# Paired i and g gates, the forget gate last, a new PSUM layout, and the shared expert's low halves on GpSimd

## The chip, the cores and the metric
One core of a Trainium2 chip. The metric is the device time of one execution in microseconds (us). TensorE (PE) multiplies, VectorE (DVE), ScalarE (ACT) and GpSimd (POOL) do elementwise work, SyncE (SP) issues DMAs. Each engine runs its own instruction list in order and waits on semaphores. TensorE and PSUM: a product accumulates in one of eight banks of 512 float32 per partition; GpSimd works on SBUF alone.

## The reference
x is [16, 256, 256] (batch B, time T, features D). Four residual layers follow each other, in float32:

```python
# RNN over T:   h = tanh(h @ Wh + x_t @ Wx + b);                    x = x + hs
# LSTM over T:  z = x_t @ Wx + b + h @ Wh   (4 x 256 columns: i, f, o, g)
#               c = sigmoid(f) * c + sigmoid(i) * tanh(g);  h = sigmoid(o) * tanh(c);  x = x + hs
# MoE:          shared = gelu(x @ sw1 + sb1) @ sw2 + sb2     (256 -> 1024 -> 256)
#               2 of 4 experts per batch row, chosen by a gate on means over T
#               x = x + sum_e w_be * mask_e * expert_e(x) + shared
# adapter:      low-rank matrices made from cond_1024, two products around a gelu;  x = x + out
```

## The kernel before
Float32 accuracy is reached with float16 matmuls: each operand is a high half (HI) and a low half (LO, the rest), and a product is W_hi x_hi + W_lo x_hi + W_hi x_lo. Features lie on the 128 partitions in C = 2 halves; B = 16 columns belong to one time step.

The scan runs in 16 blocks of U = 16 steps. In block `it`, step `u`, the engines' lists hold: LSTM step u of block it; RNN step u of block it+1; pieces of the shared expert over block it-1 as filler for TensorE; input projections for coming steps; in blocks 1 to 8 also a low-rank product (`low_rank`, steps 12 and 13), and in blocks 1 to 13 the splitting of expert weights in steps 1, 5, 7, 9 and 11 (`EXPERT_WINDOWS`). After the scan come the shared expert's last block, the routed experts and the adapter. The order within a step is written out by hand, in the four `block_steps`, one per engine.

LSTM step on TensorE (`lstm_step`, L1348): wait for the new hidden state's high half (`v_hh`); 24 matmuls of 16 columns for the tiles of f, i and g (`FIG_TILES`, L1363); wait for its low half (`v_hl`); 12 more (L1369); then 8 for o, of which four have HI and LO side by side as 32 columns, so that W_hi meets both in one matmul and the two sums lie 256 columns apart (L1374, L1378). The f, i, g sums of four steps (H = 4) share one bank of two (`FIG`), the o sums of eight steps (G = 8) one of two (`OB`). ScalarE takes one tanh over f, i and g from PSUM (`lstm_gates`, L573). VectorE then makes fc = f*c and ig = i*g (L898, L899), adds the two o sums (L901), and makes c (L904); ScalarE takes tanh of o and of c (L580, L582); VectorE makes the new hidden state's high half (L908), its float32 copy (L911), its low half (L913) and the residual add (L917). The sigmoid is a tanh of half the argument.

Ahead of these sums the projections x_t @ Wx are added into the same places, four steps at a time for f, i, g (`fig_x`) and eight for o (`o_x`). From the third use of a bank on, ScalarE writes the gate biases into it first (`seed`, L589).

The shared expert in the scan: `HALVES` says how many halves (three matmuls of 256 columns) TensorE works off in each step; `FILL` is the table made of it, jobs h0, h1, h2, d0, h3, d1, ... (hidden tile m, down tile m), and `done_tiles(u)` are the hidden tiles that end in step u. For these ScalarE makes the float32 gelu in step u (`shared_full`, L621) and its float16 high half in step u+1 (`shared_hi`, L626), both from PSUM; VectorE then makes the low half, 128x256, at the end of step u+1 (`shared_lo`, L868), and TensorE's down product waits for it. Other work at the ends of VectorE's steps: splitting x for the shared expert (L839, L842, in step 0), sums over time (L846), low halves of weights (L775), of low-rank rows (L1015, steps 2 and 4 of blocks 2 to 9), of x for the RNN (L831), and the shared expert's add (L862, step 15).

GpSimd's step (`rnn_step`, L423) belongs to the RNN: its hidden state's low half (L428), the residual add (L430), and in two of four steps the split of x for the LSTM's projections (L442, L445).

Of the kernel before, what the change touches and what calls it, by code (L numbers as in the profile page):

```python
# [54 lines left out]
FIG_TILES = [2, 3, 0, 1, 6, 7]  # L55
O_TILES = [4, 5]


def build_program(nc, a, out, scratch):
    ctx = ExitStack()  # L60
    with ctx:
# [26 lines left out]
        gate_bias = sb("gate_bias", [P, 8 + C], F32)  # L88
# [12 lines left out]
        tfig = sb("tfig", [P, 6, B], F32)  # L101
# [47 lines left out]
        FIG, OB = bank[0:2], bank[2:4]  # L149
# [8 lines left out]
        def late(*shape):  # L158
# [49 lines left out]
            ld_gate_bias p_gate_bias a_fig_seed a_o_seed pe_fig pe_o v_oz a_fig v_ig v_c2 a_tc v_hh v_h2 v_hl v_x2  # L208
            pe_h a_g v_gh v_gl pe_d v_y
# [84 lines left out]
        def _(sp):  # L294
            with nc.allow_non_contiguous_dma(reason="small tables, once"):
# [24 lines left out]
                for i, tile in enumerate(FIG_TILES + O_TILES):  # L320
                    sp.dma_start(gate_bias[:, i:i + 1], a["L1_cond_b"][tile * P:(tile + 1) * P].rearrange("(p o) -> p o", o=1)
                                 ).then_inc(s["ld_gate_bias"], 16)
# [90 lines left out]
        def _(pool):  # L413
# [42 lines left out]
            for part_, scale in ((slice(0, 4), S_LSTM), (slice(4, 6), 2 * S_LSTM), (slice(6, 8), S_LSTM)):  # L456
                nc.gpsimd.tensor_scalar(gate_bias[:, part_], gate_bias[:, part_], scale, None, ALU.mult
                                        ).then_inc(s["p_gate_bias"], 1)
            nc.gpsimd.memset(gate_bias[:, 8:8 + C], 0.0).then_inc(s["p_gate_bias"], 1)
# [3 lines left out]
            for part_ in (HI, LO):  # L463
                split_x1(T // H - 1, part_)

# [50 lines left out]
        def _(act):  # L516
# [53 lines left out]
            def lstm_gates(blk, u):  # L570
                n = blk * U + u
                act.wait_ge(s["pe_fig"], n + 1)
                nc.scalar.activation(tfig[:], FIG[u // H % 2][:, 0:6 * H * B].rearrange(  # L573
                    "p (m t b) -> p m t b", m=6, t=H)[:, :, u % H, :],
                    ACT.Tanh, scale=0.5 / S_LSTM).then_inc(s["a_fig"], 1)
# [8 lines left out]
            def seed(n_read, bank_, tiles, steps, done):  # L584

                act.wait_ge(s["a_tc"], n_read)
                n = (tiles.stop - tiles.start) * steps * B
                act.wait_ge(s["p_gate_bias"], 4)
                nc.scalar.activation(bank_[:, 0:n].rearrange("p (m t) -> p m t", t=steps * B),  # L589
                                     gate_bias[:, tiles].rearrange("p (m o) -> p m o", o=1).to_broadcast(  # L590
                                         [P, tiles.stop - tiles.start, steps * B]), ACT.Copy).then_inc(s[done], 1)

            def seeds(it, u, last):

                if u % H == H - 1 and not (last and u >= U - 2 * H):
                    seed(it * U + u + 1, FIG[u // H % 2], slice(0, 6), H, "a_fig_seed")
                if u == O_SEEDS[0] and it > 0:
                    seed(it * U, OB[1], slice(6, 8 + C), G, "a_o_seed")
                if u == O_SEEDS[1] and not last:
                    seed(it * U + G, OB[0], slice(6, 8 + C), G, "a_o_seed")  # L600
# [7 lines left out]
            def gelu(tile, m, scale, bias, banks):  # L608
                act.wait_ge(s["pe_h"], tile + 1)
                act.wait_ge(s["v_gl"], tile - 1)  # L610
# [30 lines left out]
            def block_steps(it, first, last, matrix=False):  # L641
                for u in range(U):
# [108 lines left out]
        def _(dve):  # L751


            dve.sem_inc(s["v_gl"], M)
# [110 lines left out]
            def shared_lo(tile, m):  # L865
# [3 lines left out]
                                ).then_inc(s["v_gl"], 1)  # L869

            def split_g(tile, m):
# [6 lines left out]
                                ).then_inc(s["v_gl"], 1)  # L878
# [8 lines left out]

            def lstm_step(blk, u, rnn=True):
# [4 lines left out]
                tf, ti, tg = [tfig[:, 2 * k:2 * k + 2, :].rearrange("p c b -> p (c b)") for k in range(3)]  # L893
                x = X[:, :, :, bass.ds(blk * U + u, 1)].rearrange("p c b o -> p (c b o)")
                dve.wait_ge(s["a_fig"], n + 1)
                if n:
                    dve.wait_ge(s["v_c2"], n)
                V.scalar_tensor_tensor(fc[:], tf, 1.0, c2[:], ALU.add, ALU.mult)  # L898
                V.scalar_tensor_tensor(ig[:], ti, 1.0, tg, ALU.add, ALU.mult).then_inc(s["v_ig"], 1)  # L899
                dve.wait_ge(s["pe_o"], n + 1)  # L900
                V.reduce_sum(oz[:], OB[u // G][:, :].rearrange("p (a m t b) -> p m t b a", a=2, m=C, t=G)[:, :, u % G],  # L901
                             AX_X).then_inc(s["v_oz"], 1)
# [115 lines left out]
            def block_steps(it, first, last, xr, matrix=False):  # L1018
                for u in range(U):
                    lstm_step(it, u, not last)  # L1020
                    if last and u in extras:
                        extras[u]()
                    if not first:
# [3 lines left out]
                        for m in done_tiles(u - 1) if u else ():  # L1027
                            shared_lo(it * M + m, m)
# [40 lines left out]
            tail_tile = iter(range(M))  # L1069

# [175 lines left out]
        def _(pe):  # L1246
# [101 lines left out]
            def lstm_step(blk, u):  # L1348
                n = blk * U + u
                old = (u + 1) % 2  # L1350

                def tile_at(bank_, steps, i, tile):
                    at = i * steps * B + u % steps * B
                    return bank_[:, at:at + B], tile

                fig = [tile_at(FIG[u // H % 2], H, i, tile) for i, tile in enumerate(FIG_TILES)]
                o = OB[u // G][:, :].rearrange("p (a m t b) -> p a m t b", a=2, m=C, t=G)[:, :, :, u % G]
                if not isinstance(n, int) or n > 0:
                    pe.wait_ge(s["v_hh"], n)
                for z, tile in fig:  # L1360
                    for c in range(C):
                        for h in (HI, LO):
                            MM(z, LW[:, h, 1, c, tile * P:(tile + 1) * P], LH[:, old, HI, c],  # L1363
                               start=False, stop=False, skip_group_check=True)
                if not isinstance(n, int) or n > 0:
                    pe.wait_ge(s["v_hl"], n)
                for z, tile in fig:
                    for c in range(C):
                        last = MM(z, LW[:, HI, 1, c, tile * P:(tile + 1) * P], LH[:, old, LO, c],  # L1369
                                  start=False, stop=(c == C - 1), skip_group_check=True)  # L1370
                last.then_inc(s["pe_fig"], 1)
                for i, tile in enumerate(O_TILES):
                    for c in range(C):
                        MM(o[:, 0, i], LW[:, LO, 1, c, tile * P:(tile + 1) * P], LH[:, old, HI, c],  # L1374
                           start=False, stop=False, skip_group_check=True)
                for i, tile in enumerate(O_TILES):
                    for c in range(C):
                        last = MM(o[:, :, i], LW[:, HI, 1, c, tile * P:(tile + 1) * P], LH[:, old, :, c],  # L1378
                                  start=False, stop=(c == C - 1), skip_group_check=True)
# [11 lines left out]
            def down_(tile, j, w, first, last_, ybank, halves=range(C)):  # L1391

                if 0 in halves:
                    pe.wait_ge(s["v_gl"], tile + 1)
# [37 lines left out]
            def lstm_x(bank_, i, tile, group, steps, fresh):  # L1432

                n = (steps.stop - steps.start) * B
                z = bank_[:, i * n:(i + 1) * n]
                if fresh:
                    MM(z, bias_pad[:, tile * P:(tile + 1) * P], ones_pad[:, 0:n], start=(i == 0), stop=False,
# [5 lines left out]
            def fig_x(turn, i):  # L1443

                part_ = turn % (U // H)
# [287 lines left out]
```

## Time and profile before
| what | value |
|---|---|
| median of three runs | 1118.36 us (1118.17 to 1118.6) |
| profiled execution | 1117.36 us, span 1115.4 us |
| PE busy | 1079.2 us, 97% of the span |
| DVE, ACT, POOL busy | 818.1, 586.4, 279.3 us |
| mean granted TensorE clock | 0.974 of full speed |

The span runs from the first to the last instruction. A matmul's record lasts longer than the distance to the next one, since matmuls overlap in the array; so the distance between starts is the cost of one, and a busy TensorE may still have room.

### The profile page before, as it was taken

How to read it: one execution, taken by the hardware profiler on the slowest of the kernel's cores; microseconds unless marked ns; L12 is line 12 of the kernel's file. 1: busy time of each engine (PE TensorE's matmuls, PEld its weight loads, DVE VectorE, ACT ScalarE, POOL GpSimd, SP SyncE). 2: the span in 40 equal slices, each digit the busy share in tenths (PEclk: the TensorE clock that was granted, in tenths of full speed). 3: DMA queues.
4: the chain of work that ended last, by engine and by line, in shares of the span. 5: the costliest groups of instructions: out<-in, count | busy, mean ns of one | idle time of the engine just before them, and what ended most of it. 6: DMA issues, size and time to landing. Idle time of an engine off the chain costs nothing. (4 is left out here: it accounts for less than half of the span.)

```text
span 1115.4 us, 54596 instructions
## 1 busy us (share of the span) xinstructions
PE 1079.2 (97%) x21946; PEld 979.4 (88%) x21946; DVE 818.1 (73%) x3458; ACT 586.4 (53%) x2147; POOL 279.3 (25%) x861
## 2 busy tenths in 40 slices
PE   6889999999999999999999998899999999999998
PEld 5889999999999999999999987688888888888877
DVE  7667877877877877777777676686666666676697
ACT  4456666566566566566565543433333333334486
POOL 3523323323333333333333320380000000000041
PEclk8759999999999999999999999999999999999999
DMA  8302120120220100000001110000000000000022
GB/s 258 103 23 59 56 63 25 56 65 23 61 60 26 57 18 29 14 23 23 9 4 27 16 15 12 1 2 2 2 2 2 2 1 2 2 3 2 4 90 82
DMA packets 54913, 36.91 MB, mean 33 GB/s; under 512 B 25560, under 2 KB 53514, under 8 KB 54668
## 3 DMA queue, kind: packets, MB, share of 16 engines
q1 hardware_dynamic: 54060, 33.12, 10.4%
q8 instruction: 181, 2.97, 1.1%
q14 instruction: 64, 0.52, 0.2%
q10 hardware_dynamic: 608, 0.30, 0.1%
HBM read 28.42 MB, written 4.98 MB: 30 GB/s over the span
## 5 line engine op out<-in xcount | busy, mean ns | idle before, releaser
L611 ACT ACTIVATE gel<-bank,seq 128x256 f32<-128x256 f32 x256 | 121.5, 475 | 214.7 <-PE bank L1253 211.9
L1251 PE MATMUL bank<-XHL,WE 128*128 128x256 f16 x768 | 209.9, 273 | 8.2 <-DVE XHL L842 3.4
L1251 PE MATMUL bank<-GH,WE 128*128 128x256 f16 x768 | 209.1, 272 | 2.4 <-DVE GH L868 2.0
L1253 PE MATMUL bank<-XHL,WE 128*128 128x256 f16 x768 | 209.8, 273 | 0.0
L1252 PE MATMUL bank<-XHL,WE 128*128 128x256 f16 x768 | 209.7, 273 | 0.0
L1253 PE MATMUL bank<-GH,WE 128*128 128x256 f16 x768 | 209.4, 273 | 0.0
L1252 PE MATMUL bank<-GH,WE 128*128 128x256 f16 x768 | 209.3, 273 | 0.0
L1363 PE MATMUL bank<-LH,seq 128*128 128x16 f16 x6144 | 194.4, 170 | 9.9 <-DVE LH L908 9.6
L1363 PEld LDWEIGHTS bank<-LH,seq 128*128 128x128 f16 x6144 | 171.5, 96 | 30.1 <-DVE LH L908 14.1
L428 POOL TENSOR_TENSOR RH<-rf,RH 128x32 f16<-128x32 f32 x256 | 63.7, 249 | 420.0 <-ACT RH L568 419.8
L1253 PE MATMUL bank<-seq 128*128 128x64 f16 (+2 forms) x1088 | 163.7, 208 | 0.0
L1252 PE MATMUL bank<-seq 128*128 128x64 f16 (+2 forms) x1088 | 162.4, 207 | 0.0
L1251 PE MATMUL bank<-seq 128*128 128x64 f16 (+2 forms) x1088 | 160.6, 207 | 0.0
L573 ACT ACTIVATE tfig<-bank 128x96 f32<-128x96 f32 x256 | 64.0, 250 | 173.3 <-PE bank L1369 172.3
L875 DVE CAST GH<-gel 128x256 f16<-128x256 f32 x256 | 78.2, 305 | 101.7 <-ACT gel L611 100.8
L877 DVE TENSOR_TENSOR GH<-gel,GH 128x256 f16<-128x256 f32 x256 | 113.0, 441 | 8.7
L898 DVE SCALAR_TENSOR_TENSOR fc<-tfig,c 128x32 f32<-128x32 f32 x256 | 52.1, 203 | 91.8 <-ACT tfig L573 89.2
L1369 PE MATMUL bank<-LH,seq 128*128 128x16 f16 x3072 | 114.2, 169 | 0.0
L1251 PEld LDWEIGHTS bank<-seq 128*128 128x128 f16 x1088 | 104.8, 100 | 3.4 <-issue 0.2
L1252 PEld LDWEIGHTS bank<-seq 128*128 128x128 f16 x1088 | 103.0, 100 | 3.0
L508 POOL TENSOR_TENSOR seq<-X,seq 128x512 f16<-128x512 f32 x16 | 21.4, 1343 | 332.1 <-ACT seq L694 332.1
L1253 PEld LDWEIGHTS bank<-seq 128*128 128x128 f16 x1088 | 103.9, 100 | 0.7
(210 smaller groups left out, 2641.2 us busy)
## 6 DMA issues: line engine op xcount, KB each, us to landing
stage<-in_L_cond_ew SPq DMA_DIRECT2D x64, 128.0 KB, 2.1
stage<-in_L_cond_W SPq DMA_DIRECT2D x32, 256.0 KB, 3.6
XHL<-in_x SPq DMA_DIRECT2D x8, 512.0 KB, 9.0
out<-WE SPq DMA_DIRECT2D x16, 256.0 KB, 2.2
stage<-in_L_cond_sw SPq DMA_DIRECT2D x2, 1024.0 KB, 6.2
scratch<-rows SPq DMA_DIRECT2D x96, 8.0 KB, 2.1
stage<-in_L_cond_Wx SPq DMA_DIRECT2D x1, 1024.0 KB, 9.0
stage<-in_L_cond_Wh SPq DMA_DIRECT2D x1, 1024.0 KB, 11.1
```

Of the source, the lines that this page charges most:

```text
L428: nc.gpsimd.tensor_tensor(RH[:, slot, LO], rf[:, slot], RH[:, slot, HI], ALU.subtract).then_inc(s["p_rlo"], 1)
L508: TT(X3[:, slot, LO], x, X3[:, slot, HI], ALU.subtract).then_inc(s["p_x3"], 1)
L573: nc.scalar.activation(tfig[:], FIG[u // H % 2][:, 0:6 * H * B].rearrange("p (m t b) -> p m t b", m=6, t=H)[:, :, u % H, :], ACT.Tanh, sca ...
L611: nc.scalar.activation(gel[:, m % 2, :], banks[m % len(banks)][:, 0:256], ACT.Gelu_apprx_tanh, scale=scale, bias=bias).then_inc(s["a_g"], 1)
L875: V.tensor_copy(GH[:, m % 4, HI], gel[:, m % 2]).then_inc(s["v_gh"], 1)
L877: V.tensor_tensor(GH[:, m % 4, LO], gel[:, m % 2], GH[:, m % 4, HI], ALU.subtract).then_inc(s["v_gl"], 1)
L898: V.scalar_tensor_tensor(fc[:], tf, 1.0, c2[:], ALU.add, ALU.mult)
L1251: MM(out_, w(HI), x(HI), start=start, stop=False, skip_group_check=True)
L1252: MM(out_, w(LO), x(HI), start=False, stop=False, skip_group_check=True)
L1253: return MM(out_, w(HI), x(LO), start=False, stop=stop, skip_group_check=True)
L1363: MM(z, LW[:, h, 1, c, tile * P:(tile + 1) * P], LH[:, old, HI, c], start=False, stop=False, skip_group_check=True)
L1369: last = MM(z, LW[:, HI, 1, c, tile * P:(tile + 1) * P], LH[:, old, LO, c], start=False, stop=(c == C - 1), skip_group_check=True)
```

## The change
i and g (`IG_TILES`) are now paired as o was: four times two matmuls of 16 columns with W_lo, and after the wait for the low half eight of 32 columns with W_hi on HI and LO side by side. f stays single and is finished after them; o comes last as before. That is 36 matmuls per step instead of 44. The two i, g sums are added by a new VectorE instruction (`lstm_sum`), which stands at the head of VectorE's step; the gate tanh is two, f from PSUM and i, g from SBUF. PSUM: i and g take two banks (four steps each), f and o one bank each, with four and two slots of four steps. The o projections go four steps at a time. Bias seeds: i, g and f and o each every four steps. New waits on TensorE keep a slot's writers and readers apart (`a_f`, `v_oz`, `a_f_seed`, `a_o_seed`). In the scan GpSimd makes the shared expert's low halves, between the RNN's low half and its residual add. `HALVES` is another list.

```diff
-FIG_TILES = [2, 3, 0, 1, 6, 7]
+IG_TILES = [0, 1, 6, 7]
+F_TILES = [2, 3]
 O_TILES = [4, 5]
...
-        FIG, OB = bank[0:2], bank[2:4]
+        IG, FB, OB = bank[0:2], bank[2], bank[3]
...
                 nc.gpsimd.tensor_tensor(RH[:, slot, LO], rf[:, slot], RH[:, slot, HI], ALU.subtract
                                         ).then_inc(s["p_rlo"], 1)
+                if blk > 1 and r > 0:
+                    shared_lo(blk - 1, r)
                 nc.gpsimd.tensor_tensor(x, x, rf[:, slot], ALU.add).then_inc(s["p_x1"], 1)
...
+            def shared_lo(it, u):
+
+                for m in done_tiles(u - 1):
+                    pool.wait_ge(s["a_g"], it * M + m + 1)
+                    nc.gpsimd.tensor_tensor(GH[:, m % 4, LO], gel[:, m % 2], GH[:, m % 4, HI], ALU.subtract
+                                            ).then_inc(s["g_lo"], 1)
...
             def lstm_gates(blk, u):
                 n = blk * U + u
-                act.wait_ge(s["pe_fig"], n + 1)
-                nc.scalar.activation(tfig[:], FIG[u // H % 2][:, 0:6 * H * B].rearrange(
...
+                act.wait_ge(s["pe_f"], n + 1)
...
+                nc.scalar.activation(tf[:].rearrange("p (m b) -> p m b", m=C), z[:, :, u % H], ACT.Tanh,
+                                     scale=0.5 / S_LSTM).then_inc(s["a_f"], 1)
+                act.wait_ge(s["v_zig"], n + 1)
+                nc.scalar.activation(tig[:], zig[:], ACT.Tanh, scale=0.5 / S_LSTM).then_inc(s["a_ig"], 1)
...
+            def seed_f(n):
+
+                turn = n // H
+                if n % H == 2 and 2 <= turn < TURNS - 2:
...
+            def seed_o(n):
+
+                turn = n // H
+                if n % H == 0 and 1 <= turn < TURNS - 1:
...
+            def seed_ig(n):
+
+                turn = n // H
+                if n % H == H - 1 and turn < TURNS - 2:
...
                     lstm_cell(it, u)
+                    seed_f(it * U + u)
                     if not last:
                         rnn_step(it + 1, u)
+                    seed_o(it * U + u)
                     if not first:
                         for m in done_tiles(u):
                             shared_full(it * M + m, m)
-                    seeds(it, u, last)
+                    seed_ig(it * U + u)
...
+            def lstm_sum(blk, u):
+
+                n = blk * U + u
+                dve.wait_ge(s["pe_ig"], n + 1)
+                V.reduce_sum(zig[:], IG[n // H % 2][:, :].rearrange("p (a m t b) -> p m t b a", a=2, m=NIG, t=H)[:, :, u % H],
+                             AX_X).then_inc(s["v_zig"], 1)
...
                 for u in range(U):
+                    lstm_sum(it, u)
                     lstm_step(it, u, not last)
...
-                        for m in done_tiles(u - 1) if u else ():
-                            shared_lo(it * M + m, m)
...
+                for i, tile in enumerate(IG_TILES):
                     for c in range(C):
-                        for h in (HI, LO):
...
+                        MM(z_ig[:, 0, i], w(LO, c, tile), LH[:, old, HI, c], start=False, stop=False,
+                           skip_group_check=True)
+                if u % H == 3 and 2 <= turn < TURNS - 2:
+                    pe.wait_ge(s["a_f_seed"], turn - 1)
+                for i, tile in enumerate(F_TILES):
+                    for c in range(C):
+                        MM(z_f[:, i], w(HI, c, tile), LH[:, old, HI, c], start=False, stop=False, skip_group_check=True)
+                if n > 0:
                     pe.wait_ge(s["v_hl"], n)
+                for i, tile in enumerate(IG_TILES):
                     for c in range(C):
+                        last = MM(z_ig[:, :, i], w(HI, c, tile), LH[:, old, :, c], start=False, stop=(c == C - 1),
+                                  skip_group_check=True)
+                last.then_inc(s["pe_ig"], 1)
...
+            def next_x(n):
+
+                turn = n // H + 1
+                if turn < TURNS:
+                    if n % H == 0:
+                        f_x(turn, 0)
+                        f_x(turn, 1)
+                    elif n % H == 1:
+                        o_x(turn, 0, n)
+                    elif n % H == 2:
+                        o_x(turn, 1, n)
+                        ig_x(turn, 0)
+                        ig_x(turn, 1)
+                    else:
+                        ig_x(turn, 2)
+                        ig_x(turn, 3)
...
-HALVES = [0, 3, 2, 2, 2, 2, 2, 3, 0, 3, 2, 3, 2, 3, 2, 1]
-O_STEPS = (3, 5)
+HALVES = [0, 3, 2, 2, 3, 3, 2, 3, 0, 3, 2, 3, 1, 1, 2, 2]
...
-O_SEEDS = (0, 10)
```

## Rows read from the trace of the kernel before

**Rows 1.** The page's busy times, and busy time by engine in a stretch of the routed experts.
```profile
PE 1079.2 (97%) x21946; PEld 979.4 (88%) x21946; DVE 818.1 (73%) x3458; ACT 586.4 (53%) x2147; POOL 279.3 (25%) x861
...
core 0: us, PE busy (x) PEld busy (x) DVE busy (x) ACT busy (x) POOL busy (x), PEclk, DMA share, GB/s
800.00:850.00 50.00, 50.00 (x461) 44.81 (x459) 32.03 (x91) 18.25 (x39) 0.00 (x0) 1.00 0.00 1
```

**Rows 2.** Timeline (start, duration, instruction): block 8, starts of steps 0, 1, 2, 12, 14, next block.
```profile
371.32 0.75 PE L1363 MATMUL bank<-LH,seq 128*128 128x16 f16 x24
...
373.78 0.76 PE L1363 MATMUL bank<-LH,seq 128*128 128x16 f16 x24
...
374.68 0.76 DVE L842 TENSOR_TENSOR XHL<-X,XHL 128x512 f16<-128x512 f32 x1
...
376.66 0.40 PE L1363 MATMUL bank<-LH,seq 128*128 128x16 f16 x10
...
401.64 0.76 PE L1363 MATMUL bank<-LH,seq 128*128 128x16 f16 x24
...
407.76 0.31 PE L1363 MATMUL bank<-LH,seq 128*128 128x16 f16 x6
...
412.72 0.75 PE L1363 MATMUL bank<-LH,seq 128*128 128x16 f16 x24
```

**Rows 3.** Timeline, block 8, step 4, a regular one, to the next step's start.
```profile
381.60 0.75 PE L1363 MATMUL bank<-LH,seq 128*128 128x16 f16 x24
...
381.68 0.25 DVE L913 TENSOR_TENSOR LH<-h,LH 128x32 f16<-128x32 f32 x1
...
381.85 0.20 DVE L917 SCALAR_TENSOR_TENSOR X<-h,X 128x32 f32<-128x32 f32 x1
...
382.21 0.44 PE L1369 MATMUL bank<-LH,seq 128*128 128x16 f16 x12
382.30 0.41 DVE L868 TENSOR_TENSOR GH<-gel,GH 128x256 f16<-128x256 f32 x1
...
382.69 0.25 ACT L573 ACTIVATE tfig<-bank 128x96 f32<-128x96 f32 x1 [0.40 <-PE bank L1369]
...
383.08 0.18 DVE L899 SCALAR_TENSOR_TENSOR ig<-tfig 128x32 f32<-128x32 f32 x1
383.18 0.22 DVE L901 TENSOR_REDUCE oz<-bank 128x32 f32<-128x64 f32 x1
383.32 0.18 DVE L904 SCALAR_TENSOR_TENSOR c<-fc,ig 128x32 f32<-128x32 f32 x1
...
383.82 0.19 DVE L908 SCALAR_TENSOR_TENSOR LH<-to,tc 128x32 f16<-128x32 f32 x1 [0.18 <-ACT tc L582]
...
384.07 0.58 PE L1363 MATMUL bank<-LH,seq 128*128 128x16 f16 x17
```

**Rows 4.** Groups of instructions by line (count, busy us, mean ns, idle before), whole execution.
```profile
L626 ACT ACTIVATE GH<-bank,sb 128x256 f16<-128x256 f32 x128 | 59.9, 468 | 0.0
L775 DVE SCALAR_TENSOR_TENSOR WE<-stage,WE 128x256 f16<-128x256 f32 x80 | 39.9, 500 | 3.2 <-ACT WE L529 3.2
L529 ACT ACTIVATE WE<-stage 128x256 f16<-128x256 f32 x80 | 32.4, 406 | 0.0
...
L846 DVE TENSOR_REDUCE blocksum<-X 128x16 f32<-128x256 f32 x32 | 12.9, 408 | 0.0
L1015 DVE SCALAR_TENSOR_TENSOR rows<-low_f,rows 128x128 f16<-128x128 f32 x16 | 12.2, 764 | 0.0
L862 DVE SCALAR_TENSOR_TENSOR X<-bank,X 128x512 f32<-128x512 f32 x16 | 10.8, 678 | 2.4 <-PE bank L1253 2.4
L673 ACT ACTIVATE rows<-low_f 128x256 f16<-128x256 f32 x8 | 10.7, 1337 | 0.0
```

**Rows 5.** Timeline behind the scan: GpSimd's 128x256 operations beside VectorE's L868.
```profile
708.85 0.66 POOL L472 TENSOR_TENSOR seq<-seq,eb 128x256 f32<-128x256 f32 x1
708.93 1.72 DVE L868 TENSOR_TENSOR GH<-gel,GH 128x256 f16<-128x256 f32 x2
709.59 0.79 POOL L476 TENSOR_TENSOR seq<-seq 128x256 f32<-128x256 f32 x1
```

More of the change, by code:

```diff
@@ L464, in _ @@
                 split_x1(T // H - 1, part_)
+            for u in range(1, U):
+                shared_lo(NB - 1, u)
             pool.wait_ge(s["v_oh"], 1)
@@ L1349, in lstm_step @@
                 n = blk * U + u
+                turn = n // H
                 old = (u + 1) % 2
[L1352 to L1358, printed above, removed]
+                w = lambda h, c, tile: LW[:, h, 1, c, tile * P:(tile + 1) * P]
@@ L1366, in lstm_step @@
+                for i, tile in enumerate(F_TILES):
+                    for c in range(C):
+                        MM(z_f[:, i], w(HI, c, tile), LH[:, old, HI, c], start=False, stop=False, skip_group_check=True)
+                if n > 0:
                     pe.wait_ge(s["v_hl"], n)
-                for z, tile in fig:
+                for i, tile in enumerate(IG_TILES):
                     for c in range(C):
-                        last = MM(z, LW[:, HI, 1, c, tile * P:(tile + 1) * P], LH[:, old, LO, c],
-                                  start=False, stop=(c == C - 1), skip_group_check=True)
@@ L1371, in lstm_step @@
-                last.then_inc(s["pe_fig"], 1)
+                        last = MM(z_ig[:, :, i], w(HI, c, tile), LH[:, old, :, c], start=False, stop=(c == C - 1),
+                                  skip_group_check=True)
+                last.then_inc(s["pe_ig"], 1)
+                for i, tile in enumerate(F_TILES):
+                    for c in range(C):
+                        MM(z_f[:, i], w(LO, c, tile), LH[:, old, HI, c], start=False, stop=False, skip_group_check=True)
+                        last = MM(z_f[:, i], w(HI, c, tile), LH[:, old, LO, c], start=False, stop=(c == C - 1),
+                                  skip_group_check=True)
@@ L1372, in lstm_step @@
+                last.then_inc(s["pe_f"], 1)
+                if u % H == 1 and 1 <= turn < TURNS - 1:
+                    pe.wait_ge(s["a_o_seed"], turn)
                 for i, tile in enumerate(O_TILES):
                     for c in range(C):
-                        MM(o[:, 0, i], LW[:, LO, 1, c, tile * P:(tile + 1) * P], LH[:, old, HI, c],
-                           start=False, stop=False, skip_group_check=True)
+                        MM(z_o[:, 0, i], w(LO, c, tile), LH[:, old, HI, c], start=False, stop=False,
+                           skip_group_check=True)
@@ L1376, in lstm_step @@
                 for i, tile in enumerate(O_TILES):
                     for c in range(C):
-                        last = MM(o[:, :, i], LW[:, HI, 1, c, tile * P:(tile + 1) * P], LH[:, old, :, c],
-                                  start=False, stop=(c == C - 1), skip_group_check=True)
+                        last = MM(z_o[:, :, i], w(HI, c, tile), LH[:, old, :, c], start=False, stop=(c == C - 1),
+                                  skip_group_check=True)
                 last.then_inc(s["pe_o"], 1)
@@ L1528, in block_steps @@
                                 shared_down(it - 1, m, halves)
[L1529 to L1537 removed]
+                    next_x(it * U + u)
                     if matrix:
```

145 lines of the change are left out of this document (79 added, 66 removed).

## The prediction

> **What bounds the kernel now.** I read the page's busy shares first, then TensorE's step starts on the timeline, then one step on all engines. TensorE counts as busy for 97% of the span [rows 1], which is no bound by itself, since its records overlap. The last 400 us (routed experts, adapter) really are TensorE back to back, 461 matmuls in 50 us, 0.108 us each [rows 1]; the change doesn't touch them. The change lies in the 256 LSTM steps, 16 blocks of 16. A full block with a low-rank product lasts 412.72 - 371.32 = 41.40 us [rows 2].
>
> A regular step shows the chain [rows 3], in us from its first matmul at 381.60. TensorE's first pass of 24 matmuls takes 0.61 (0.025 each), the low-half pass starts at 0.61, its last matmul at 0.885; ScalarE's gate tanh starts at 1.09, 0.21 after that; VectorE's i*g product at 1.48, the o sum at 1.58, c at 1.72, the new hidden state at 2.22; the next step starts at 2.47. Nothing in that row of events waits for anything but the one before it, so a regular step is 2.47 of latency. 16 x 2.47 = 39.5; the other 1.9 us of the block are 0.41 in step 1 (373.78 to 376.66 is 2.88), 1.18 in steps 12 and 13 (401.64 to 407.76 is 6.12) [rows 2], and small change.
>
> **The change, part by part.** *TensorE.* 44 LSTM matmuls per step become 36, 0.2 us less at 0.025. That shortens a regular step only if the chain gets shorter too. The o projections become twice as many with half the columns, which I cost at nothing; the DMAs are the same.
>
> *The chain of a regular step.* Twelve matmuls now stand ahead of the wait for the low half: 0.30. The low half starts at 0.08 and lasts 0.25 [rows 3], so TensorE sees it at about 0.38, a new stall of 0.08. Eight paired matmuls: the last starts at 0.56, and with the same 0.21 VectorE can start the new sum at 0.78. No row has that sum (64 out of 128 in). It lies between the o sum (64 in, 0.22) [rows 3] and the 256-in reduction (0.41) [rows 4]; by their slope 0.28. Ends: 0.22 and 0.41. It ends at 1.06; with 0.04 of hand-over the tanh of the i and g gates starts at 1.10, lasts 0.24 (the old one 0.25), and i*g starts at 1.38 instead of 1.48. The forget gate (eight more matmuls, tanh from 0.98 for 0.21) is ready before. From i*g on nothing changes: 2.37, 0.10 less. Over 256 steps that would be 26 us.
>
> *VectorE's queue.* The gain needs VectorE free at 0.78, where before it was needed at about 1.37 (1.09 + 0.25 + 0.03). All that the step before left in its queue stands ahead of the new sum, behind the residual add that starts at 0.25 and lasts 0.20 [rows 3]. A weight piece (0.50) [rows 4] just fits, since the start of one record overlaps the end of the last. These don't: in step 1 the split's subtraction ends at 1.66 (374.68 + 0.76 - 373.78) [rows 2], so the sum starts 0.84 late; in steps 3 and 5 of blocks 2 to 9 the low-rank low half (0.76) [rows 4] runs from 0.38 to 1.14, 0.29 late each; in step 0 the shared expert's add (0.68) [rows 4], 0.2 late. Smaller ones (12 to 15) I leave out.
>
> *ScalarE's queue.* The new HALVES put the shared expert's high half (0.47) into steps 2, 3, 4, 5, 7, 8, 11, 12; steps 5, 7 and 11 have an expert's weight piece too (0.41) [rows 4], which before never met it. Started at 1.23 behind the gate tanh, both end at about 2.0, so the o tanh and, behind it, the cell tanh come 0.25 late: 0.75 per block. In step 2 the second hidden tile waits for a bank that this high half frees at 1.70, with three projection tiles after it instead of two: 0.25. In step 9 the o seed, now made there behind the late RNN tanh, costs 0.35 on TensorE's new seed wait. The low-rank high half (1.34) [rows 4] in step 14, behind the f seed, now reaches 0.35 into step 15's tanh.
>
> *Steps 12 and 13.* They lose 16 LSTM matmuls (0.40) and nine of 256 columns (0.97): 6.12 falls to 4.75, two chains. The low-rank product still stands behind the o projection's new wait for the o sum; 0.35 remains.
>
> Without GpSimd's work a block is 16 x 2.37 = 37.9, + 0.84 + 0.58 + 0.2 + 0.75 + 0.25 + 0.35 + 0.35 + 0.35 = 41.6, against 41.4. In blocks without low-rank work 0.58 and twice 0.35 fall away: 40.3, against 41.40 - 1.18 = 40.2. So this half of the change is near nothing: 8 x 0.2 + 6 x 0.1 = +2.2, and block 0, which has no fill and no such queues, gives 16 x 0.1 = 1.6 back; the last block I take as unchanged: +0.6 us.
>
> *GpSimd's low halves.* A 256-wide subtraction on GpSimd takes 0.66 [rows 5], on VectorE 0.41 in a quiet place [rows 3]. GpSimd has the time, and it makes the RNN's low half first, so its in-order queue delays only the residual add and the split behind it, which the RNN's lead of a block hides. The cost is at VectorE: where two of its 256-wide subtractions met GpSimd's 256-wide operations (0.66 and 0.79) they took 1.72 together, 0.86 each [rows 5] against 0.41, so +0.45. The work starts at about 0.24 of the steps after u = 2, 3, 4, 5, 7, 8, 11 and 12, beside VectorE's residual add at 0.25 and whatever stands behind it, all ahead of the new sum. Ends: nothing (VectorE gets through first and its next operation, the sum, reads PSUM), and 0.66 per meeting. I take 0.40, by the row that has this very shape, where another wide two-input operation follows the add: steps 6, 8, 12 and 13, and 3 and 5 in the eight low-rank blocks; and 0.1 in the remaining two or four. That is 6 x 0.4 + 2 x 0.1 = 2.6 in eight blocks and 4 x 0.4 + 4 x 0.1 = 2.0 in six: 20.8 + 12.0 = 32.8 us. What VectorE loses of work here (eight times 0.41) had no place in the chain before: it lay between 0.5 and 1.37.
>
> The Trainium skill (SBUF — State Buffer, "Who interferes with whom") says that a VectorE instruction with two SBUF inputs and a GpSimd instruction that reads SBUF exclude each other for the whole of the first one, whichever started first. The trace agrees in the place above, where VectorE's operation starts 0.08 behind GpSimd's and ends after it. By that rule alone each meeting costs what is left of GpSimd's instruction, at most 0.66, and the time is that of the second rival.
>
> **Sum.** The profiled execution took 1117.4 us (span 1115.4 and 2.0 around it), 1.0 below the median of 1118.4. 1117.4 + 0.6 + 32.8 = 1150.8; I say 1151.
>
> **Rivals.** *VectorE is free in time (faster).* If the new sum really starts at 0.78 in nearly all steps, because the tails overlap better than their durations say and GpSimd yields, only step 1 (0.84) and 0.35 in steps 12 and 13 are left: 37.9 + 1.2 = 39.1 in eight blocks (-2.3) and 38.8 in six (-1.4), 1117.4 - 18 - 9 - 2 = 1088; with half of that gain 1103. It decides at the start of the sum: under about 1.0 on the mean of the steps the chain gains. For it: in the regular step VectorE's tail ends at 1.11 (382.30 + 0.41), and the subtraction that ends it is the one that leaves the engine. Against it: step 1 shows that VectorE's tail already reaches the chain at the later place.
>
> *The ports lock in full.* Every GpSimd subtraction stops the next two-input operation for 0.66, in the 6 x 8 + 4 x 6 = 72 meetings with a wide one: 1151 + 72 x 0.26 = 1170. For it: the 0.86 pairs; against it: in the regular step the same two engines meet in the residual adds and VectorE's took only 0.20 [rows 3].
>
> *GpSimd slips between.* VectorE wins most meetings, 0.1 each: 14 x 8 x 0.1 = 11, so 1129; with none, 1118, no change.
>
> *No effect of the pairing:* if TensorE was the bound, 0.2 us x 256 would show as 51 us less, 1066. The regular step with only two halves of fill is 2.47 all the same, so I leave it 3%.
>
> **Chances.** Forecast (1136 to 1163) 0.43; full lock (above) 0.14; slip, slower 0.15; no change 0.06; faster 0.22 (1088 to 1116, the 3% of the pairing among it). A difference of 0.2% is about what can be told from none here. So slower 0.72, same 0.06, faster 0.22. The range leaves out the far parts of the faster case and of the full lock: 1100 to 1172; the likeliest case's own is 1136 to 1163.
>
> **What would show it.** Right: regular steps (6 or 10 apart from queues) of 2.37, step 1 of about 3.2, the new sum of 0.28 at 0.78 after the step's start where the queue is empty and behind 1.0 where GpSimd's subtraction runs; VectorE's residual add or weight piece stretched beside it; TensorE idle ahead of the paired matmuls. Wrong: blocks under 40 us, or residual adds that stay at 0.20 beside GpSimd's 0.66.

## The result and the profile after

The changed kernel takes 1164.64 us (median of 4 runs, 1162.86 to 1165.75) beside 1118.48 (4 runs, 1118.17 to 1119.08): ratio 1.0411, 95% interval 1.0393 to 1.0429, slower. The forecast was 1151: the time lies inside the stated range (1100 to 1172), but 1.6 above the range of the likeliest case (1136 to 1163). Its profiled execution took 1162.86 us, 45.5 more than the one of before (1117.4).

The page of the changed kernel; the second row is the granted clock of TensorE in tenths, in 40 slices of 29 us:

```profile
PE 1074.0 (93%) x20286; PEld 947.1 (82%) x20286; DVE 874.9 (75%) x3594; ACT 648.5 (56%) x2495; POOL 359.2 (31%) x983
...
PEclk8659999999999999999899999899999999999999
```

TensorE has 1660 matmuls less than in [rows 1] and is busy for 5 us less; VectorE is busy for 57 us more, with 136 more instructions. The last hidden state of the scan begins at 740.86 instead of 695.43: 45.4 of the 45.5 us are lost inside the scan. Against the blocks of before, block 0 loses 3.4 us, block 1 1.3, blocks 2 to 9 (which have the low-rank halves) 23.9, blocks 10 to 14 (the late blocks) 13.8, the last block 3.1. Block 8, which answers to [rows 2], lasts 437.68 - 393.34 = 44.34 us where 41.4 stood:

```profile
393.34 0.36 PE L1411 MATMUL bank<-LH,seq 128*128 128x16 f16 x8
...
437.68 0.36 PE L1411 MATMUL bank<-LH,seq 128*128 128x16 f16 x8 [0.36 <-DVE LH L956]
```

**A regular step.** Timeline of the changed kernel, block 8, step 10, to the next step's start (answers to [rows 3]; L931 is the new sum):

```profile
421.44 0.36 PE L1411 MATMUL bank<-LH,seq 128*128 128x16 f16 x8
...
421.69 0.20 DVE L965 SCALAR_TENSOR_TENSOR X<-h,X 128x32 f32<-128x32 f32 x1
421.81 0.49 DVE L814 SCALAR_TENSOR_TENSOR WE<-stage,WE 128x256 f16<-128x256 f32 x1
...
421.83 0.36 PE L1422 MATMUL bank<-LH,seq 128*128 128x32 f16 x8
...
422.23 0.28 DVE L931 TENSOR_REDUCE zig<-bank 128x64 f32<-128x128 f32 x1
...
422.84 0.19 DVE L946 SCALAR_TENSOR_TENSOR ig<-tig 128x32 f32<-128x32 f32 x1
...
423.58 0.19 DVE L956 SCALAR_TENSOR_TENSOR LH<-to,tc 128x32 f16<-128x32 f32 x1 [0.18 <-ACT tc L606]
...
423.83 0.36 PE L1411 MATMUL bank<-LH,seq 128*128 128x16 f16 x8
```

The paired matmuls (L1422) start at 0.39 of the step (forecast 0.38), the sum at 0.79, it lasts 0.28, i*g starts at 1.40, and the step lasts 2.39. A weight piece (L814) ahead of the sum just fits. So far the change does what it says.

**A step with GpSimd's low half.** The same kernel, block 8, step 4, which has the same chain and a 0.41 reduction (L885) in VectorE's queue; L448 is GpSimd's new work:

```profile
404.35 0.36 PE L1411 MATMUL bank<-LH,seq 128*128 128x16 f16 x8
...
404.58 0.67 POOL L448 TENSOR_TENSOR GH<-gel,GH 128x256 f16<-128x256 f32 x1
404.60 0.73 DVE L965 SCALAR_TENSOR_TENSOR X<-h,X 128x32 f32<-128x32 f32 x1
...
404.73 0.36 PE L1422 MATMUL bank<-LH,seq 128*128 128x32 f16 x8
...
405.25 0.41 DVE L885 TENSOR_REDUCE blocksum<-X 128x16 f32<-128x256 f32 x1
...
405.58 0.27 DVE L931 TENSOR_REDUCE zig<-bank 128x64 f32<-128x128 f32 x1
```

The residual add (L965) is recorded 0.02 behind GpSimd and takes 0.73 instead of 0.20: it ends only behind GpSimd's. The reduction behind it starts 0.53 later than it could, and the sum at 1.23 instead of 0.79. The paired matmuls had long been done.

Over the whole execution (groups by line: count, busy us, mean ns, idle before) GpSimd's low half takes 0.70 and the residual add 0.30 on the mean:

```profile
L448 POOL TENSOR_TENSOR GH<-gel,GH 128x256 f16<-128x256 f32 x120 | 84.1, 701 | 28.1 <-ACT GH L663 28.1
...
L965 DVE SCALAR_TENSOR_TENSOR X<-h,X 128x32 f32<-128x32 f32 x256 | 77.9, 304 | 0.0
...
L814 DVE SCALAR_TENSOR_TENSOR WE<-stage,WE 128x256 f16<-128x256 f32 x80 | 48.1, 602 | 4.1 <-ACT WE L550 3.9
```

The weight pieces, 0.50 in [rows 4], take 0.60. Where VectorE's add gets through (0.20), the next operation with two SBUF inputs is held instead. In step 6 of block 6 (step start 320.56) that is the weight piece, with 0.90, and the sum starts at 1.19:

```profile
320.79 0.75 POOL L448 TENSOR_TENSOR GH<-gel,GH 128x256 f16<-128x256 f32 x1
...
320.81 0.20 DVE L965 SCALAR_TENSOR_TENSOR X<-h,X 128x32 f32<-128x32 f32 x1
320.93 0.90 DVE L814 SCALAR_TENSOR_TENSOR WE<-stage,WE 128x256 f16<-128x256 f32 x1
```

The add runs beside a low half 84 times, and there are only these two outcomes: 41 times it takes 0.73 and GpSimd 0.67, 43 times it takes 0.20 and GpSimd 0.75. The start times do not tell them apart: the add is recorded 0.012 to 0.017 us behind GpSimd in all 84.

### The profile page after: what moved, and what is told of

It reads as the page before. It is cut to its first block and busy times, and to the rows that moved or that the text cites. A ratio compares the mean times of both kernels' runs of the same rounds, so it can differ in the third digit from the quotient of the medians.

```text
span 1160.9 us, 52385 instructions
## 1 busy us (share of the span) xinstructions
PE 1074.0 (93%) x20286; PEld 947.1 (82%) x20286; DVE 874.9 (75%) x3594; ACT 648.5 (56%) x2495; POOL 359.2 (31%) x983
## 5 line engine op out<-in xcount | busy, mean ns | idle before, releaser
L436 POOL TENSOR_TENSOR RH<-rf,RH 128x32 f16<-128x32 f32 x256 | 69.6, 272 | 387.1 <-ACT RH L589 387.0
L1300 PE MATMUL bank<-seq 128*128 128x64 f16 (+2 forms) x1216 | 167.6, 205 | 20.6 <-DVE oz L949 19.7
L1302 PE MATMUL bank<-seq 128*128 128x64 f16 (+2 forms) x1216 | 168.3, 205 | 0.0
L1301 PE MATMUL bank<-seq 128*128 128x64 f16 (+2 forms) x1216 | 168.1, 205 | 0.0
L1300 PEld LDWEIGHTS bank<-seq 128*128 128x128 f16 x1216 | 116.7, 101 | 38.4 <-issue 24.6
L1411 PE MATMUL bank<-LH,seq 128*128 128x16 f16 x2048 | 92.1, 171 | 32.1 <-DVE LH L956 27.4
L596 ACT ACTIVATE tf<-bank 128x32 f32<-128x32 f32 x256 | 51.9, 203 | 120.6 <-PE bank L1428 120.0
L1301 PEld LDWEIGHTS bank<-seq 128*128 128x128 f16 x1216 | 115.5, 101 | 2.5
L1411 PEld LDWEIGHTS bank<-LH,seq 128*128 128x128 f16 x2048 | 69.5, 97 | 58.2 <-DVE LH L956 52.2
L1302 PEld LDWEIGHTS bank<-seq 128*128 128x128 f16 x1216 | 115.9, 101 | 0.8
L599 ACT ACTIVATE tig<-zig 128x64 f32<-128x64 f32 x256 | 66.4, 259 | 51.2 <-DVE zig L931 48.6
L956 DVE SCALAR_TENSOR_TENSOR LH<-to,tc 128x32 f16<-128x32 f32 x256 | 50.8, 198 | 58.5 <-ACT tc L606 58.5
```

Of the source, the lines that this page charges most:

```text
L596: nc.scalar.activation(tf[:].rearrange("p (m b) -> p m b", m=C), z[:, :, u % H], ACT.Tanh, scale=0.5 / S_LSTM).then_inc(s["a_f"], 1)
L599: nc.scalar.activation(tig[:], zig[:], ACT.Tanh, scale=0.5 / S_LSTM).then_inc(s["a_ig"], 1)
L956: V.scalar_tensor_tensor(hh, to[:], 1.0, tc[:], ALU.add, ALU.mult).then_inc(s["v_hh"], 1)
L1300: MM(out_, w(HI), x(HI), start=start, stop=False, skip_group_check=True)
L1301: MM(out_, w(LO), x(HI), start=False, stop=False, skip_group_check=True)
L1302: return MM(out_, w(HI), x(LO), start=False, stop=stop, skip_group_check=True)
```

## The experiments

Two theories were on trial from the start. **A**: the time goes to VectorE's queue ahead of the new sum, which GpSimd's low halves stretch. **B**: it goes elsewhere (the new order on TensorE and ScalarE, the new waits), and the stretched instructions are hidden. From e5 on, the expectations say what the two mean for the place in question.

**e1, the residual add ahead of GpSimd's low half.**
```diff
-                if blk > 1 and r > 0:
-                    shared_lo(blk - 1, r)
                 nc.gpsimd.tensor_tensor(x, x, rf[:, slot], ALU.add).then_inc(s["p_x1"], 1)
+                if blk > 1 and r > 0:
+                    shared_lo(blk - 1, r)
```


> The changed kernel with one swap on GpSimd: the RNN's residual add goes ahead of the shared expert's low half. Theory A (a GpSimd operation with SBUF inputs that starts first holds VectorE's two-input operations until it ends): VectorE's residual add, at 0.25 of a step, then meets GpSimd's 0.27 add again instead of its 0.67 subtraction, the new sum starts at 0.79 instead of 0.95 to 1.34 in steps 3, 4, 6, 8 and 12, so about 0.16 + 0.4 + 3 x 0.4 less per block, 14 blocks: 25 us, about 1140. Theory B (the loss lies in VectorE's and ScalarE's own queues and TensorE's clock, GpSimd's order does not matter): 1160 to 1166.

Measured 1147.28 (1141.96 to 1150.27), ratio 1.0274 (1.0255 to 1.0293): 17 us of the loss are gone, by nothing but the order of two GpSimd instructions. Timeline, block 8, step 4:
```profile
391.62 0.36 PE L1411 MATMUL bank<-LH,seq 128*128 128x16 f16 x8
...
391.87 0.21 DVE L965 SCALAR_TENSOR_TENSOR X<-h,X 128x32 f32<-128x32 f32 x1
391.99 0.41 DVE L885 TENSOR_REDUCE blocksum<-X 128x16 f32<-128x256 f32 x1
...
392.16 0.67 POOL L448 TENSOR_TENSOR GH<-gel,GH 128x256 f16<-128x256 f32 x1
...
392.41 0.29 DVE L931 TENSOR_REDUCE zig<-bank 128x64 f32<-128x128 f32 x1
```
GpSimd's 0.67 now begins 0.31 later in the step, beside the reduction, which has one input from SBUF and keeps its 0.41; the sum is back at 0.79. The time is between A's and B's numbers, since other places remain: on the mean of blocks 2 to 8 the sum of step 12 is still at 1.10, and step 9 still 2.81 long.

**e2, the low halves back on VectorE**, at the ends of its steps as before; the rest of the change stays.
```diff
-                if blk > 1 and r > 0:
-                    shared_lo(blk - 1, r)
...
+                        for m in done_tiles(u - 1) if u else ():
+                            shared_lo(it * M + m, m)
```


> The changed kernel with the low halves in the scan back on VectorE, at the end of its steps as before. Theory A: 0.41 to 0.47 in VectorE's queue fits ahead of the new sum where it stands alone (steps 3, 4, 9) and delays it by about 0.4 where it follows a weight piece, an x low half or a low-rank half, so no gain in steps 6, 8, 12, 13 and 5, only in 3 and 4: 14 x 0.5 = 7 us less, about 1157. Theory B: VectorE's queue is the loss, so 3.5 us more per block: 1190 or more. If the port costs nothing and the queue neither: 1130.

Measured 1161.21 (1155.59 to 1162.99), ratio 1.0395 (1.0376 to 1.0415): hardly better than GpSimd's. GpSimd has no low half here that could hold VectorE, but the 128x256 subtraction itself stands ahead of the sum. Timeline, block 8, step 12 (L903 is the low half):
```profile
420.79 0.36 PE L1407 MATMUL bank<-LH,seq 128*128 128x16 f16 x8
...
421.04 0.21 DVE L961 SCALAR_TENSOR_TENSOR X<-h,X 128x32 f32<-128x32 f32 x1
421.16 0.49 DVE L903 TENSOR_TENSOR GH<-gel,GH 128x256 f16<-128x256 f32 x1
...
421.58 0.41 DVE L810 SCALAR_TENSOR_TENSOR WE<-stage,WE 128x256 f16<-128x256 f32 x1
...
421.91 0.28 DVE L927 TENSOR_REDUCE zig<-bank 128x64 f32<-128x128 f32 x1
```
The sum starts at 1.12. So the pairing pulls VectorE's tail onto the chain, whoever makes the low halves.

**e3, GpSimd writes only.** It writes zeros in place of the subtraction, which leaves the shared expert's low halves in the scan out of the result.
```diff
-                    nc.gpsimd.tensor_tensor(GH[:, m % 4, LO], gel[:, m % 2], GH[:, m % 4, HI], ALU.subtract
-                                            ).then_inc(s["g_lo"], 1)
+                    nc.gpsimd.memset(GH[:, m % 4, LO], 0.0).then_inc(s["g_lo"], 1)
```


> The changed kernel, but in the scan GpSimd only fills the low halves with zeros (same tile, same place, no SBUF input); the low halves of the shared expert's activations are left out. Theory A: nothing to hold VectorE's second input, all new sums of steps 3, 4, 6, 8, 12 at 0.79 to 0.82, 14 blocks x 2.4 = 33 us less: about 1131. Theory B: 1160 to 1166. If a GpSimd write alone holds VectorE too: between.

Measured 1124.62 (1123.61 to 1126.32), ratio 1.0063 (1.0045 to 1.008). The same waits, order and instruction counts, and 40 us less. Timeline, block 8, step 4 (begins at 384.34):
```profile
384.56 0.31 POOL L448 MEMSET GH<- 128x256 f16 x1
...
384.59 0.21 DVE L964 SCALAR_TENSOR_TENSOR X<-h,X 128x32 f32<-128x32 f32 x1
384.71 0.41 DVE L884 TENSOR_REDUCE blocksum<-X 128x16 f32<-128x256 f32 x1
...
385.12 0.29 DVE L930 TENSOR_REDUCE zig<-bank 128x64 f32<-128x128 f32 x1
```
The add lies beside GpSimd's instruction and keeps its 0.21; the sum is at 0.78. GpSimd's instruction is shorter too (0.31 instead of 0.67), but the add is not held even for what is left of that: beside the memset it takes 0.205 on the mean of 84. Blocks 2 to 9 take 40.97 on the mean, 0.3 less each than before; block 0 still loses 3.6, the last block 2.4. B falls for the 40 us; the 6.7 us that are left in e3's scan do lie elsewhere.

**e4, the kernel before with the low halves on GpSimd**, and nothing else of the change.
```diff
+                if blk > 1 and r > 0:
+                    shared_lo(blk - 1, r)
                 nc.gpsimd.tensor_tensor(x, x, rf[:, slot], ALU.add).then_inc(s["p_x1"], 1)
...
-                        for m in done_tiles(u - 1) if u else ():
-                            shared_lo(it * M + m, m)
```


> The kernel before with one part of the change alone: GpSimd makes the low halves in the scan, between the RNN's low half and its residual add. Its VectorE is needed only at 1.37 of a step. Theory A: the held residual add ends at 0.98, a weight piece at 1.45, a low-rank half at 1.75: 0 to 0.3 in steps 3 and 5 of eight blocks and little elsewhere, 1119 to 1126. A rival, that the held operation costs its 0.5 wherever it falls: 120 x 0.5 = 60 us, 1175.

Measured 1125.29 (1124.75 to 1126.07), ratio 1.0069 (1.0052 to 1.0086). Groups by line:
```profile
L928 DVE SCALAR_TENSOR_TENSOR X<-h,X 128x32 f32<-128x32 f32 x256 | 86.2, 337 | 0.0
L440 POOL TENSOR_TENSOR GH<-gel,GH 128x256 f16<-128x256 f32 x120 | 84.3, 703 | 29.9 <-ACT GH L637 29.9
```
The residual adds are held even more often (53 times beside a low half; 0.337 on the mean, 0.254 in the kernel before), and it costs 7 us instead of 40. The holding is the same; what differs for VectorE is that it was needed at 1.37 of a step here, and is at 0.79 in the changed kernel. e4 also keeps the fill (`HALVES`) of the kernel before; e3, which has the new one, loses 6.7 us in all.

**e5, matmuls in TensorE's gap ahead of step 13.** The granted clock falls to half nine times between 342 and 742 us of the changed kernel, for 3.4 or 6.8 us. Windows around one of the falls (length; busy us and count of PE, weight loads, DVE, ACT, POOL; granted clock; DMA):
```profile
518.00:520.00 2.00, 1.14 (x25) 0.75 (x23) 1.62 (x12) 1.35 (x6) 0.99 (x5) 0.98 0.00 0
520.00:523.40 3.40, 3.40 (x71) 3.03 (x71) 2.46 (x12) 1.30 (x8) 1.52 (x5) 0.51 0.02 5
523.40:526.00 2.60, 2.57 (x77) 2.37 (x74) 1.91 (x11) 1.46 (x7) 0.47 (x2) 1.00 0.00 0
```
TensorE was busy for 1.14 of the 2.00 us ahead of the fall. Against the same steps of blocks without a fall, the steps hit by the falls are about 5 us longer in all (step 15 of blocks 10 to 12 takes 3.38 to 3.42, of blocks 13 and 14 2.42 and 2.33). The edit adds matmuls with a zero operand:
```diff
+        zeros = sb("zeros", [P, B], F16)
...
+            V.memset(zeros[:], 0.0)
...
+                    if u == 13:
+                        pe.wait_ge(s["v_zig"], n)
+                    for i in range(12 if u == 13 else 0):
+                        MM(z_ig[:, 0, i % NIG], w(HI, 0, IG_TILES[i % NIG]), zeros[:, :], start=False, stop=False,
+                           skip_group_check=True)
```


> The changed kernel with 12 more matmuls of 16 columns (stationary tile as in the step, moving operand zeros, so nothing is added to the gates) ahead of step 13's wait for the hidden state, in every block: 0.30 us of TensorE work where its own idle time ahead of step 13 is 0.18 to 0.89. Theory A: the nine falls of the granted clock in the scan, which cost the steps that they hit 5.2 us in all, follow from TensorE standing idle there, so that with the gap filled most of them go; step 13 itself does not get longer by more than 0.1. 1164.6 - 5.2 = 1159.4, with 16 x 0.1 at most back: 1159 to 1161. Theory B: the falls have another reason (the other engines' load, or the phase of the program): as many as before, 1164 to 1166.

Measured 1157.1 (1153.04 to 1158.38), ratio 1.0342 (1.0317 to 1.0367). The time is just below A's, its reason is not: there are again nine falls, and by the same comparison they cost about 5 us again (step 15 of blocks 10 to 13 takes 3.08 to 3.42, of block 14 2.34). The 7.5 us came from elsewhere: the add is held beside 12 low halves instead of 41, its mean fell from 304 to 238 ns, and step 4 of blocks 10 to 12 from 2.82 to 2.39. Twelve matmuls on another engine changed who is held at 0.24 of a step. On what causes the falls e5 is inconclusive, since TensorE still stands idle there: ahead of step 13 for 0 to 0.47 us (0.18 to 0.89 before the edit), and within step 13 for 0.5 to 1.0.

**e6, the expert's weight pieces moved.**
```diff
-        EXPERT_WINDOWS = (1, 5, 7, 9, 11)
+        EXPERT_WINDOWS = (1, 6, 9, 10, 13)
```


> The changed kernel with the expert's weight pieces in steps 1, 6, 9, 10, 13 instead of 1, 5, 7, 9, 11: no piece then shares a step with a shared high half on ScalarE, and on VectorE none stands ahead of a sum that GpSimd's low half delays. Theory A (the forecast's step on ScalarE, 0.25 each in steps 5, 7 and 11; the trace has 0.17, 0.11 and 0.23 over a regular 2.39): 14 x 0.51 = 7.1 less, and about 0.05 less in each of the locked steps 6, 8 and 12, 14 x 0.15 = 2.1: 1155 to 1158. Theory B: ScalarE's cell tail is hidden and these steps are longer for TensorE's fill, which has no idle time before steps 8 and 12: 1163 to 1166.

Measured 1142.18 (1139.58 to 1145.55), ratio 1.0211 (1.0191 to 1.023): 22 us less, more than either theory had. ScalarE's part is near what was expected (steps 5, 7 and 11 of late blocks fall from 2.59, 2.50, 2.62 to 2.52, 2.34, 2.46, together 0.39 of the 0.51). The surprise is in steps 6, 8 and 12, for which 0.05 was expected. Step 12 of block 6, changed kernel (step start 336.65):
```profile
336.88 0.67 POOL L448 TENSOR_TENSOR GH<-gel,GH 128x256 f16<-128x256 f32 x1
336.90 0.73 DVE L965 SCALAR_TENSOR_TENSOR X<-h,X 128x32 f32<-128x32 f32 x1
...
337.55 0.51 DVE L814 SCALAR_TENSOR_TENSOR WE<-stage,WE 128x256 f16<-128x256 f32 x1
...
337.98 0.28 DVE L931 TENSOR_REDUCE zig<-bank 128x64 f32<-128x128 f32 x1
```
and in e6 (step start 330.07):
```profile
330.31 0.75 POOL L448 TENSOR_TENSOR GH<-gel,GH 128x256 f16<-128x256 f32 x1
...
330.32 0.21 DVE L965 SCALAR_TENSOR_TENSOR X<-h,X 128x32 f32<-128x32 f32 x1
...
330.86 0.29 DVE L931 TENSOR_REDUCE zig<-bank 128x64 f32<-128x128 f32 x1 [0.33 <-PE bank L1422]
```
The two differ in who is held as well as in the piece, so all steps 6, 8 and 12 of blocks 1 to 13 count. In the changed kernel, with the piece, the sum starts on the mean at 1.34 where the add is held (18 steps) and at 1.19 where the piece is (20); in e6, without it, at 0.90 where the add is held (8) and at 0.80 where it is not (31). Against 0.79 in the same steps of e3, where nothing is held, a meeting costs 0.01 to 0.1 by itself and 0.4 to 0.55 with a wide operation behind it.

**e7, shorter queues everywhere**: e1's order, e6's windows, the o seed ahead of the RNN's tanh, the last add of the shared expert one step later, and the two long VectorE operations cut into quarters.
```diff
...
+QUARTERS = (7, 12, 14)
-SPLIT_WINDOWS = (0, 0, 3, 13)
+SPLIT_WINDOWS = (0, 0, 3, 11)
...
-ADD_WINDOW, HI_WINDOW, LO_LATER = 13, 14, (2, 4)
+ADD_WINDOW, HI_WINDOW, LO_LATER = 13, 14, (2, 4, 5, 8)
```


> The residual add ahead of GpSimd's low half (as e1), the pieces in steps 1, 6, 9, 10, 13, the o seed ahead of the RNN tanh, the last block's add of the shared expert at the end of step 15, and the two long VectorE operations cut up: the block's split by quarters in steps 7, 12, 14 and 0, the low-rank low half by quarters in steps 2, 4, 5, 8. Theory A (the chain through VectorE's and ScalarE's queues is what is left): from 1147.3 go 14 x 0.7 for step 1, 14 x 0.35 for step 9, 14 x 0.5 for steps 5, 7 and 11, 8 x 0.3 for the low-rank steps and 2.5 for the last block, 26.6: 1118 to 1126. Theory B (TensorE, which already runs into steps 3, 7, 8, 11 and 15 without a gap, takes over): 1130 to 1140.

Measured 1137.42 (1135.77 to 1137.7), ratio 1.0173 (1.0156 to 1.019): B's range, though not by B alone. Step 1 fell from 3.17 to 2.63 and the last block from 44.9 to 43.1, but a cut piece that lands beside a low half is held too (step 8: a split's subtraction of 0.29 takes 0.66, the step 2.91), and in steps 5 and 8 TensorE now comes straight from its fill and starts 0.12 to 0.13 late. No kernel here beats the one before.

## Why the forecast came out as it did

The direction and the mechanism were right, the price was 13.8 us too low. The profiled execution lies 12 us above the forecast; about half of that is in GpSimd's low halves (32.8 forecast, about 39 measured) and half in the rest of the change (0.6 forecast, 6.7 measured).

The mean over blocks 2 to 8 of the changed kernel and of e3, worked out from the timelines: the sum's start after the step's start (VectorE's L956 + 0.25), and the step's length from L956 to L956.

| step | changed: sum, length | e3: sum, length | forecast of GpSimd's cost | measured (difference) |
|---|---|---|---|---|
| 1 | 1.58, 3.17 | 1.58, 3.17 | 0 | 0 |
| 3 | 0.95, 2.56 | 0.95, 2.56 | 0.40 | 0 |
| 4 | 1.17, 2.76 | 0.79, 2.39 | 0.1 | 0.37 |
| 5 | 1.32, 3.23 | 0.83, 2.62 | 0.40 | 0.61 |
| 6 | 1.26, 2.88 | 0.79, 2.46 | 0.40 | 0.42 |
| 8 | 1.28, 2.87 | 0.79, 2.39 | 0.40 | 0.48 |
| 9 | 0.73, 2.81 | 0.73, 2.43 | 0.1 | 0.38 |
| 12 | 1.29, 2.88 | 0.78, 2.39 | 0.40 | 0.49 |
| 13 | 1.34, 2.92 | 0.89, 2.48 | 0.40 | 0.44 |

**The chain of a regular step**: right. 2.37 was forecast, 2.39 measured; the sum at 0.78 for 0.28, measured 0.79 for 0.28. The slope between the two sums of before gave the right price here.

**VectorE's queue.** Step 1 was forecast with the sum 0.84 late, measured 0.79 late (3.17). The low-rank low halves were forecast at 0.29 late in steps 3 and 5; e3 has 0.17 and 0.04, and in step 3 the late blocks, which have no low-rank work, show the same 0.95: that is TensorE's fill, not VectorE.

**ScalarE's queue.** Steps 5, 7 and 11 were forecast at +0.25 each; in late blocks they are 2.59, 2.50 and 2.62, and moving the pieces takes off 0.07, 0.16 and 0.16. The term was sized 0.09 to 0.18 too large. Step 2 was forecast +0.25 and is +0.06. Step 9 was forecast +0.35 for the new o seed wait, and is +0.42, which is luck, for the reason is another. Its timeline in the changed kernel (step start 418.63):
```profile
419.70 0.67 POOL L448 TENSOR_TENSOR GH<-gel,GH 128x256 f16<-128x256 f32 x1
...
419.75 0.26 PE L1435 MATMUL bank<-LH,seq 128*128 128x16 f16 x4 [0.23 <-ACT bank L612]
...
419.84 0.58 DVE L944 SCALAR_TENSOR_TENSOR fc<-tf,c 128x32 f32<-128x32 f32 x1 [0.19 <-ACT tf L596]
...
420.34 0.30 DVE L946 SCALAR_TENSOR_TENSOR ig<-tig 128x32 f32<-128x32 f32 x1
```
The seed wait is there (0.23 on TensorE), but GpSimd's low half, late in this step, holds f*c for 0.58. e2 and e3 keep the seed where it is and have 2.42 and 2.43; e7 moves the seed and keeps the 2.81.

**The half without GpSimd** was forecast at +0.6 us; e3 has 6.7 in its scan. Inside the full blocks the forecast is near: blocks 2 to 9 -2.3 (forecast +1.6), block 1 -0.5 and blocks 10 to 14 +3.4 (+0.6 for the six). That is partly luck. A block was forecast at 41.6 and takes 40.97, from terms that miss both ways: steps 0, 14 and 15 are 0.85 over three regular ones (forecast 0.2 + 0.35), steps 12 and 13 0.1 (0.35), step 10, which has no term, 0.2. And 2.9 of the +3.4 have no term either: they lie in step 15 of blocks 11, 13 and 14, where the granted clock fell to its lower level and which takes 3.38 to 3.40, against 2.42 in blocks 10 and 12. The other misses are at the two ends. Block 0 was to gain 1.6 and loses 3.4 in the changed kernel. TensorE's waits there (us, times, longest) and the window of the block:
```profile
PE bank L1300 <- DVE oz L949: 4.5, 6, 1.1
...
PE bank L1497 <- DVE oz L949: 1.4, 2, 0.7
```
```profile
41.00:84.60 43.60, 33.81 (x890) 31.60 (x887) 32.32 (x171) 24.95 (x119) 13.09 (x46) 0.54 0.15 48
```
The o projections' new wait for the o sum, which the forecast took as covered by the fill, has no cover in block 0, because there is no fill; and behind it TensorE's projections run at a mean clock of 0.54 (0.58 in block 0 before). The clock has a part in it: in e2 steps 1 to 3 of block 0 ran mostly at the higher level and took 3.14, 2.40 and 2.42 instead of 3.48, 2.60 and 2.93, about 1.0 less. It is not the whole: block 0 of e2 has no more time at the lower level than the one of before (32.6 and 33.3 us) and is 2.3 longer all the same. The wait itself keeps two engines apart that use one bank, so taking it away was not tried: that this wait makes the rest is read from the rows, not shown. The last block was taken as unchanged and loses 3.1: about 1.4 in steps 3 to 8 (0.5 of it in e3 too), 0.5 in step 1, whose causes stay open, and 0.7 in step 15 (4.30 against 3.56). There VectorE's add of the shared expert at the end of step 14 waits for TensorE's fill of step 15 (at the lower clock until 738.3), and the new sum of step 15 stands behind it (step start 736.80):
```profile
738.91 0.69 DVE L901 SCALAR_TENSOR_TENSOR X<-bank,X 128x512 f32<-128x512 f32 x1 [1.71 <-PE bank L1302]
739.51 0.28 DVE L931 TENSOR_REDUCE zig<-bank 128x64 f32<-128x128 f32 x1
```
e7 lets that add wait until the end of step 15, among its other edits; its step 15 takes 2.38, and its last block is 1.7 shorter than the changed kernel's.

**GpSimd's low halves** were forecast at 32.8 us and cost about 39 (45.4 - 6.7 in the scans; 1164.64 - 1124.62 = 40.0 by the medians). This is the mechanism of the forecast, under-priced: 20.8 forecast for blocks 2 to 9 and about 26.2 measured, while the 12.0 for the six other blocks are met (12.1). A meeting with a wide operation behind the add was put at 0.40, measured 0.42 to 0.49 in steps 6, 8, 12 and 13 and 0.61 in step 5; step 3 costs nothing, since TensorE's fill keeps its sum at 0.95 with GpSimd or without; step 4 was put at 0.1 because the operation behind the add there is a reduction, which is not held but stands behind the held add all the same (0.37); step 9 meets the low half later, at f*c.

The Trainium skill (SBUF — State Buffer, "Who interferes with whom") has the two instructions exclude each other for the whole of the first one. It also says that a GpSimd instruction which only writes does not contend with a VectorE instruction that has two SBUF inputs; e3 bears that out, with the add at 0.21 beside the memset's 0.31. The rows agree on the lock too: in each of the 84 meetings one of the two is held, the add (0.73 beside GpSimd's 0.67) or GpSimd's (0.75 beside the add's 0.20). Who was first cannot be read from the start times, which have GpSimd ahead in all of them.

The rival of a full lock (1170) is right that one of the two always waits, but its price did not come out: a held add is 0.53 longer and a held weight piece 0.40, not 0.66, and 72 meetings at 0.66 with the others at 0.1 make 51.5 us for GpSimd's part, where about 39 were measured. That 1170 is only 5 above the time is luck, since the half without GpSimd, 6.1 too low, takes back half of that. The faster rival falls at its own test: the mean start of the sum over blocks 2 to 8 is 1.08, behind its 1.0.

**An assumption that no rival named.** The text said that VectorE loses eight times 0.41 of work that "had no place in the chain before". True of the kernel before; with the new sum it has one: e2 shows 37.2 us lost in its profiled scan with the low halves on VectorE and none on GpSimd. So the change has no good place for them: of 45.4 us about 7 come without any low half made in the scan, and about 39 from making them on GpSimd. On VectorE they cost some 30 by e2's profiled execution (37.2 - 6.7), which was 5.6 us faster than its median, and 36.6 by the medians (1161.21 - 1124.62).

## What to carry to other kernels

When a change shortens a chain by putting a new step on an engine early in its period, list what that engine does between its last step of the chain and the new one: all of it moves from slack onto the path, here some 0.4 to 0.6 us in six of sixteen steps (4, 5, 6, 8, 12, 13) for a gain of 0.1. Work handed to GpSimd is not off VectorE if both read two SBUF operands: what the handover costs is the held time plus the queue behind the held instruction, so look at what stands behind it, and at the order of GpSimd's own instructions (one swap was worth 17 us). Price the first and the last block by themselves: here they lost 6.5 us of which the forecast had none.

## What the runs showed of the hardware

When VectorE's add and GpSimd's 128x256 subtraction, both with two SBUF inputs, start within 0.02 us of each other, one of them is held, and the profiled start times do not tell which: GpSimd is recorded first in all 84 meetings, the add is held in 41 of them in the changed kernel and in 12 in e5, whose edit is on TensorE. So small edits elsewhere move the time by several us (e5: 7.5).

TensorE's granted clock falls to its lower level (1.2 GHz) for 3.4 or 6.8 us inside the scan of the changed kernel, of e1 to e3 and of e5 to e7, all with the new matmul order, and once for 17.1 us at the end of e3's; the first of them come between 342 and 532 us. In e4 the first comes at 664 us, in the kernel before at 693. In the 2 us ahead of each fall inside the scans of the changed kernel, e3 and e5, TensorE stood idle for 0.4 to 1.3 us. Shortening one of its gaps (e5) left as many falls. What sets them off stays open.
